# First attention: Q and K rows held as two 16-bit parts each, scores by three 16-bit products, opening rows moved from two queues

## The reference

```python
xh = x.reshape(B, S, H, dh)                       # H = 16 heads, dh = 16
theta_q = xh / (1.0 + jnp.abs(w_q)) + b_q + t * phi_q
sin_q, cos_q = lookup_sin_cos(theta_q)            # table of 1024, linear in between
Q = jnp.concatenate([cos_q, sin_q], axis=-1)      # 32 wide; K alike
theta_v = xh / (1.0 + jnp.abs(w_v)) + b_v
V = cos_v + sin_v
scores = jnp.einsum('bqhd,bkhd->bhqk', Q, K) / scale
scores = jnp.where(causal, -jnp.inf, scores)
attn = jax.nn.softmax(scores, axis=-1)
out = jnp.einsum('bhqk,bkhd->bqhd', attn, V).reshape(B, S, D)
theta_out = out / (1.0 + jnp.abs(w_out)) + b_out
return cos_o + sin_o                              # x = x + this, x normalised before
```

## Time and profile before

| | |
|---|---|
| median of three runs | 1050.36 us |
| the profiled execution | 1049.52 us |
| its span (first to last instruction) | 1047.6 us |
| PE busy | 912.2 us (87%) |
| DVE busy | 716.4 us (68%) |
| ACT busy | 574.1 us (55%) |
| scores' fills, line 635, busy | 123.6 us |
| weighings, line 655, busy | 74.6 us |
| exponentials, line 542, busy | 137.5 us |

### The profile page before, as it was taken

One profiled execution on the slowest core, in us unless ns is written; L12 is line 12 of the kernel. 1 busy time (PEld: TensorE's weight loads), 2 busy tenths in 40 slices (PEclk: granted clock), 3 DMA queues, 4 the chain that ended last, 5 costly groups with the idle time before them and its releaser, 6 DMA issues. The chain is left out here.

```text
span 1047.6 us, 20337 instructions
## 1 busy us (share of the span) xinstructions
PE 912.2 (87%) x7994; PEld 561.8 (54%) x7994; DVE 716.4 (68%) x1404; ACT 574.1 (55%) x1030; POOL 299.6 (29%) x293
## 2 busy tenths in 40 slices
PE   1587989799579789999789999998799988999997
PEld 0232333333147545565456777776689974455554
DVE  7986774615678989887768889886678764344412
ACT  3478688878478553552145555554678753332410
POOL 1222333212137231000237667666153210000000
PEclk9997889899779999999989999999899999999999
DMA  5406050320131030000130000000200000000001
GB/s 153 72 1 81 1 74 8 45 38 1 50 113 41 2 131 1 2 2 1 34 131 2 3 2 2 2 2 2 71 2 2 2 2 1 1 6 16 21 1 41
DMA packets 20573, 30.34 MB, mean 29 GB/s; under 512 B 5936, under 2 KB 15870, under 8 KB 19328
## 3 DMA queue, kind: packets, MB, share of 16 engines
q1 hardware_dynamic: 18368, 26.96, 11.2%
q10 hardware_dynamic: 2112, 2.10, 0.6%
HBM read 18.56 MB, written 2.10 MB: 20 GB/s over the span
## 5 line engine op out<-in xcount | busy, mean ns | idle before, releaser
L542 ACT ACTIVATE t_pT<-t_sc 128x1536 f32<-128x1536 f32 x96 | 137.5, 1454 | 48.9 <-PE t_sc L635 48.1
L635 PE MATMUL t_sc<-t_qk 32*128 32x512 f32 (+3 forms) x768 | 123.6, 603 | 43.7 <-DMA t_qk<-t_sines 26.0
L3149 PE MATMUL f_psh<-f_h,fs_w 128*128 128x512 f16 x512 | 114.4, 379 | 1.5 <-DVE f_h L3093 1.5
L3093 DVE SCALAR_TENSOR_TENSOR f_h<-f_psh,f_h 128x512 f16<-128x512 f32 x64 | 43.8, 690 | 100.8 <-ACT f_h L3119 100.7
L635 PEld LDWEIGHTS t_sc<-t_qk 32*128 32x128 f32 x768 | 56.6, 209 | 102.3 <-ACT t_pT L542 47.0
L261 POOL TENSOR_SCALAR_AFFINE_SELECT t_pT<-t_pT 128x512 f32<-128x512 f32 x64 | 61.2, 977 | 170.5 <-ACT t_pT L542 170.3
L3119 ACT ACTIVATE f_h<-f_psh 128x512 f16<-128x512 f32 x64 | 38.2, 597 | 108.4 <-PE f_psh L3149 108.4
L2612 POOL TENSOR_SCALAR_AFFINE_SELECT r_att<-r_att 128x1024 f16<-128x1024 f16 x64 | 69.5, 1108 | 68.5 <-DVE r_att L2652 68.3
L655 PE MATMUL t_ot<-t_pT,t_v 128*17 128x512 f32 (+3 forms) x768 | 74.6, 505 | 10.1 <-DVE t_ou L394 8.5
L3149 PEld LDWEIGHTS f_psh<-f_h,fs_w 128*128 128x128 f16 x512 | 49.8, 98 | 59.0 <-issue 2.0
L1908 PE MATMUL c_pso<-ck_VO,c_pT 128*128 128x256 f16 x480 | 55.0, 273 | 1.4 <-DVE c_pT L1759 1.4
(11 more groups left out here) (510 smaller groups left out, 2056.2 us busy)
## 6 DMA issues: line engine op xcount, KB each, us to landing
t_qk<-t_cosines SPq DMA_DIRECT2D x24, 128.0 KB, 5.6
t_qk<-t_sines SPq DMA_DIRECT2D x24, 128.0 KB, 7.0
x<-in_x ACTq DMA_DIRECT2D x4, 512.0 KB, 6.8
out_x<-x SPq DMA_DIRECT2D x4, 512.0 KB, 2.9
r_rcos<-in_ret_cos SPq DMA_DIRECT2D x1, 1280.0 KB, 8.0
r_rsin<-in_ret_sin SPq DMA_DIRECT2D x1, 1280.0 KB, 10.6
t_qk<-t_cosines SPq DMA_DIRECT2D x16, 64.0 KB, 2.3
t_qk<-t_sines SPq DMA_DIRECT2D x16, 64.0 KB, 2.3
```

The costliest lines, as they stand in the source:

```text
L542: a.activation(pT[:, at:at + 3, :].rearrange("p a s -> p (a s)"), sc[s % 2][:], ACT.Exp, scale=CURVE * CURVE / math.sqrt(2 * DH)).then_inc ...
L635: last = t.matmul(sc[s % 2][:, 512 * k + at:512 * k + at + w], qk[r, g % 3, 1, P * i:P * i + P], qk[r, g % 3, 0, q0:q0 + w], start=(part = ...
L3093: v.scalar_tensor_tensor(dst[:, 1], psh[:, i % BANKS, :], 0.0, dst[:, 0], ALU.max, ALU.subtract).then_inc(lo_done, 1)
L3149: last = mm(psh[:, i % BANKS, :], l, r, start=(k == 0), stop=(k == len(todo) - 1))
```

## The change

`cosines` and `sines` are still formed in 32 bits. Each is then split into two 16-bit parts, the value rounded to 16 bits and what is left over, in the new tiles `cos_parts` and `sin_parts`; `qk` holds both parts of each row (the bytes stay the same). A score is the sum of three 16-bit products: high by high, high of K by low of Q, low of K by high of Q.

- In group 0 ACT makes the rounded parts, in the later groups DVE does; DVE subtracts in all.
- In group 0 the four transfers of quad 0's sines are issued by ACT, those of the second half behind exp 1; all others stay with SP.
- `turn_step(1)` moves from before exp 8 to before exp 3 of quad 0, and `prepare(1)` with its rest moves ahead of `post_v(0)` and `pre_v(1)`. Statistics of the second batch, the row gains and `variances(1)` change places around `post_qk(0, 1)`.
- `turn_step(n)` on ACT now waits for `bent` instead of the transfers; `post_qk(n)` waits for the transfers out of the parts before it writes them.

```diff
-        qk = sb("qk", [P, 3, 2, S])
+        qk = sb("qk", [P, 3, 2, 2, S], F16)
+        cos_parts, sin_parts = sb("cos_parts", [P, 2, 2, S], F16), sb("sin_parts", [P, 2, 2, S], F16)
...
-        TURN_AT = {(0, 8): 1, (2, 2): 2, (4, 2): 3}
+        TURN_AT = {(0, 3): 1, (2, 2): 2, (4, 2): 3}
...
+        def moves(g, c, lo, hi):
+
+            for hh in range(4):
+                at, to = 64 * (g % 2) + 16 * hh, 32 * hh + 16 * c
+                yield qk[to:to + 16, g % 3, :, :, lo:hi], (cos_parts, sin_parts)[c][at:at + 16, :, :, lo:hi]
...
             for h in range(2):
                 for g in range(2):
                     for c in range(2):
-                        if g == 0:
-                            sp.wait_ge(bent, 2 * pieces_of(0, h) - 1 + c)
+                        if g == 0 and c == 1:
+                            continue
+                        sp.wait_ge(bent, 2 * pieces_of(0, h) - 1 + c)
                         move(g, c, 512 * h, 512 * h + 512, moved[g] if h or g else first)
...
             def post_qk(n, h=None):
                 f = piece(frac, h)
+                lo, hi = (0, S) if h is None else (512 * h, 512 * h + 512)
                 v.wait_ge(sin_pre, pieces_of(n, h))
-                for w, waves in ((cosines, cos_waves), (sines, sin_waves)):
+                if n:
+                    parts_free(n)
+                sides = ((cosines, cos_waves, cos_parts), (sines, sin_waves, sin_parts))
+                for w, waves, _ in sides:
                     v.wait_ge(waves, pieces_of(n, h))
-                    v.scalar_tensor_tensor(piece(w, h), f, CURVE_OFF, piece(w, h), ALU.add, ALU.mult).then_inc(bent, 1)
+                    v.scalar_tensor_tensor(piece(w, h), f, CURVE_OFF, piece(w, h), ALU.add, ALU.mult).then_inc(formed, 1)
+                if n:
+                    v.wait_ge(formed, 2 * pieces_of(n, h))
+                    for w, _, parts in sides:
+                        v.tensor_copy(parts[:, :, 0, lo:hi], cut(w, lo, hi)).then_inc(rounded, 1)
+                for c, (w, _, parts) in enumerate(sides):
+                    v.wait_ge(rounded, 2 * pieces_of(n, h) - 1 + c)
+                    v.tensor_tensor(parts[:, :, 1, lo:hi], cut(w, lo, hi), parts[:, :, 0, lo:hi], ALU.subtract).then_inc(bent, 1)
...
+            sums(1, 0, 3, 4)
+            sums(1, 1, 4, TB)
 
             for h in range(2):
...
                 if h == 0:
                     post_qk(0, 0)
-            sums(1, 0, 3, 4)
-            sums(1, 1, 4, TB)
+            post_qk(0, 1)
+            variances(1)
             v.wait_ge(s_row, 16 * 4)
             row_gains(0, 0, 1, slice(0, 128))
-            post_qk(0, 1)
-            variances(1)
             pre_v(0)
+            prepare(1)
+            prepare_rest(1)
+            post_v(0)
             row_gains(0, 0, 1, slice(128, D))
+            pre_v(1)
             row_gains(1, 2, 3, slice(0, D))
             v.wait_ge(rs_ready, 2)
             v.wait_ge(mean_ready, 2)
             normalise(TB, 2 * TB, xn_next)
-            post_v(0)
-            pre_v(1)
-            prepare(1)
-            prepare_rest(1)
...
+            def move_sines(h):
+
+                a.wait_ge(bent, 2 * pieces_of(0, h))
+                for dst, src in moves(0, 1, 512 * h, 512 * h + 512):
+                    a.dma_start(dst, src).then_inc(moved[0] if h else first, 16)
...
-            waves_qk(0, 0)
-            waves_qk(0, 1)
+            for h in range(2):
+                waves_qk(0, h)
+                for c, (w, parts) in enumerate(((cosines, cos_parts), (sines, sin_parts))):
+                    a.wait_ge(formed, 2 * pieces_of(0, h) - 1 + c)
+                    a.copy(parts[:, :, 0, 512 * h:512 * h + 512],
+                           w[:].rearrange("p (k s) -> p k s", k=2)[:, :, 512 * h:512 * h + 512]).then_inc(rounded, 1)
+                if h == 0:
+                    move_sines(0)
             for g in range(QUADS):
                 for e in range(EXPS):
...
                     exp_step(EXPS * g + e)
+                    if (g, e) == (0, 1):
+                        move_sines(1)
...
-                for part in range(2):
+                for part, (of_k, of_q) in itertools.product(range(2), ((0, 0), (0, 1), (1, 0))):
                     for slot, h, k in chunks:
...
-                            last = t.matmul(sc[s % 2][:, 512 * k + at:512 * k + at + w], qk[r, g % 3, 1, P * i:P * i + P],
-                                            qk[r, g % 3, 0, q0:q0 + w], start=(part == 0), stop=True, skip_group_check=True)
+                            last = t.matmul(sc[s % 2][:, 512 * k + at:512 * k + at + w], qk[r, g % 3, 1, of_k, P * i:P * i + P],
+                                            qk[r, g % 3, 0, of_q, q0:q0 + w], start=(part == 0 and of_k == of_q == 0),
+                                            stop=(of_k == 1), skip_group_check=True)
```

More of the change, by code:

```diff
@@ L1 @@
 from contextlib import ExitStack
+import itertools
 import math
@@ L155, in table_attention @@
         cos_pre, sin_pre, cos_waves, sin_waves, bent = (sem(n) for n in ("cos_pre", "sin_pre", "cos_waves", "sin_waves", "bent"))
+        formed, rounded = sem("formed"), sem("rounded")
         first, moved = sem("first"), [sem(f"moved{k}") for k in range(3)]
@@ L217, in move @@
             def move(g, c, lo, hi, done):
[L219 to L222, removed]
+                for dst, src in moves(g, c, lo, hi):
+                    sp.dma_start(dst, src).then_inc(done, 16)
             for h in range(2):
@@ L349, in post_qk, with cut, parts_free @@
                 f = piece(frac, h)
+                lo, hi = (0, S) if h is None else (512 * h, 512 * h + 512)
                 v.wait_ge(sin_pre, pieces_of(n, h))
-                for w, waves in ((cosines, cos_waves), (sines, sin_waves)):
+                if n:
+                    parts_free(n)
+                sides = ((cosines, cos_waves, cos_parts), (sines, sin_waves, sin_parts))
+                for w, waves, _ in sides:
                     v.wait_ge(waves, pieces_of(n, h))
-                    v.scalar_tensor_tensor(piece(w, h), f, CURVE_OFF, piece(w, h), ALU.add, ALU.mult).then_inc(bent, 1)
+                    v.scalar_tensor_tensor(piece(w, h), f, CURVE_OFF, piece(w, h), ALU.add, ALU.mult).then_inc(formed, 1)
[6 more added lines that the diff above has]
+                    v.tensor_tensor(parts[:, :, 1, lo:hi], cut(w, lo, hi), parts[:, :, 0, lo:hi], ALU.subtract).then_inc(bent, 1)
+            def cut(w, lo, hi):
+                return w[:].rearrange("p (k s) -> p k s", k=2)[:, :, lo:hi]
+            def parts_free(n):
+                for g in (2 * n - 2, 2 * n - 1):
+                    v.wait_ge(moved[g % 3], moves_of(g))
+                if n == 1:
+                    v.wait_ge(first, 16 * 8)
             def pre_v(n):
@@ L476, in _ @@
             prepare_rest(1)
+            post_v(0)
+            row_gains(0, 0, 1, slice(128, D))
+            pre_v(1)
+            row_gains(1, 2, 3, slice(0, D))
+            v.wait_ge(rs_ready, 2)
+            v.wait_ge(mean_ready, 2)
+            normalise(TB, 2 * TB, xn_next)
             for g in range(1, QUADS):
@@ L524, in turn_step @@
                 if n:
[L525 to L528, removed]
+                    a.wait_ge(bent, 2 * pieces_of(n - 1))
                 lo, hi = (0, S) if h is None else (512 * h, 512 * h + 512)
```

## The result

The changed kernel took 1058.01 us (median of 14 runs, 1053.80 to 1062.26), the kernel before 1049.67 in the same comparison (14 runs, 1045.51 to 1055.47). The ratio is 1.0071, 95% interval [1.0048, 1.0095]: slower. The forecast was 1063, in a range of 1050 to 1076. The profiled execution took 1058.36 us (span 1056.6), against 1049.52 (span 1047.6).

A forecast was written before the change was run, and what follows sets the result against it. TensorE was taken as the bound in plain stretches, the vector engine then TensorE in odd quads; 5.5 + 6.9 + 4.9 + 5.0 - 1.75 - 2.2 - 5.5 = +12.9 on 1049.52 gave 1062.4, forecast 1063 us, range 1050 to 1076.

The forecast's parts named there:

- opening, up to T: Up to T, the start of the first odd quad's cosine activation: +3.4 to +8.7 us later, taken as +5.5.
- stop, quad 1: First odd quad, slot 2: TensorE waits for the vector engine to empty the second output bank; stage 6.9 us later.
- stop, quad 3: Second odd quad: TensorE waits for the same bank, after a slack of 2.4 us; stage 4.9 us later.
- clock behind the stops: After both new stops TensorE runs 8 us at half clock: 2.5 us lost twice, 5.0 in all.
- fills after quads 1, 3, 5: Shorter score fills give back 2.2 us after g = 2, 1.75 after g = 4, 5.5 from g = 5 on.
- stage end: End of the first attention, at about 275 us before the change: +12.9 us as the sum of all terms.
- The four operations: Two casts and two subtractions of 128x2048 in post_qk on the vector engine, ahead of the bank's emptying: 7.3 us.
- the third load bare: Rival: each fill's third weight load isn't overlapped, 0.2 to 0.3 us per fill; no gain, 1074 us; chance 0.08.
- The six slots: TensorE's weighing slots in the opening, before T: 5.35 us at full clock, at most 10.7 at half.
- The second queue saving nothing: Opening: issuing sines' transfers from the scalar engine too saves nothing, as it is busy when the data come.
- Rows of quad 6: Rows of Q and K arrive later at quad 6, where it is close: counted as nothing, up to 1 us.
- The faster rival: Slot 2 of quads 1 and 3: the vector engine's four operations hide, so -9 us, 1041 us; chance 0.12.

The follow-up runs named there:

- bank_first: Changed kernel with front_o(g-1, 1) moved ahead of pre_v(n+1) in odd quads; 1048.79 us, ratio 0.9975 to the kernel before.
- value_between: Changed kernel with post_v(0) moved between prepare(1) and prepare_rest(1) in the opening; 1059.90 us, ratio 1.0088 to the kernel before.

## Why the prediction was right, and where it was off

The direction, the place and the mechanism were right; the forecast was 5 us too high, and the terms of the stage were 8 too high, of which a late start of the profiled execution hides 2.5. By its own terms, in the profiled executions:

| term | predicted | measured | from |
|---|---|---|---|
| opening, up to T | +5.5 | +5.0, of it 2.5 not the kernel's | T 84.44 against 79.46 |
| stop, quad 1 | +6.9 | +7.0 | T to slot 2: 24.73 against 17.76 |
| stop, quad 3 | +4.9 | +4.8 | 24.53 against 19.72 |
| clock behind the stops | +5.0 | -0.3 | see below |
| fills after quads 1, 3, 5 | -2.2, -1.75, -5.5 | -2.9, -0.9, -5.4 | |
| stage end | +12.9 | +7.3 | 282.58 against 275.32 |
| span | | +9.0 | 1056.6 against 1047.6 |

**The step that failed is the clock behind the stops.** The prediction took 8 us at half clock behind each stop, after the 10 us seen at 146 to 156: 4 us of lost work less six shorter fills. It was 4.4 and 3.6 us, some 2 us of lost work each, and the shorter fills paid for that: from slot 2 to the activation of the next rotation it took 10.83 us against 10.84 in quad 1 (predicted 2.5 more) and 10.55 against 10.85 in quad 3. In the row that the prediction used, the stop was 4.2 us long and the clock fell only at its end:

```profile
145.50:146.00 0.50, 0.00 (x0) 0.00 (x0) 0.47 (x2) 0.50 (x1) 0.00 (x0) 0.98 1.11 180
```

So all of the 10 us at 0.50 lay in work there (9.71 of 10 us busy). In the two new, longer stops the clock fell 1.8 and 4.2 us after TensorE stopped, and 5.8 and 3.2 us at 0.50 passed while it stood anyway. The Trainium skill ("TensorE: Matmul & The Clock Gate", Part 1) says that the window in which activity is watched is free-running. By that rule the time at half clock behind a stop depends on where the stop falls, which would fit the three stops; no run here isolates it.

**Where the stage and the total differ.** The stage ends 7.3 us later and the span 9.0. The 1.7 us arise in stages that the change doesn't touch. From the stage end to the end of the span the thirteen profiled executions take between 771.4 and 776.8 us with the same code, so 1.7 is within what single executions differ by. Since 2.5 us of the profiled opening is not the kernel's and the medians still differ by 8.3, the profiled execution and the medians don't add up to better than some 3 us.

**The four operations** took 8.0 us in quad 1 and 7.6 in quad 3 by starts (predicted 7.3): casts 1.23 and 1.65 in quad 1, 1.23 and 1.22 in quad 3, subtractions 2.71. The cast was priced about right, the subtraction 0.36 too low. The bank was predicted free at T + 24.6 and was at T + 24.67; that it is so close is in part luck. In quad 1 the four took 0.7 us and `post_v` 0.4 us more than assumed, and `pre_v` 1.2 us less than before (7.57 against 8.74).

**The fills** were forecast at 0.89 and 1.6, and were 0.82 and 1.46. The rule of the Trainium skill ("TensorE: Matmul & The Clock Gate", Part 3), that loads overlap only with matmuls of another row group, would have left the third load bare. The trace does not agree. Nine products and nine loads in 0.82 us show nothing bare, and a fourth product adds 0.22, one matmul of 512 columns; the rival falls.

**The opening** was the second term that was mis-sized, 5.5 us against 2.5 of the kernel's own; the late start made it look right. Exp 2's fill was forecast at 45.9 and came at 45.55, or 43.1 without the late start. The reason failed: the prediction put the sines' issue on the scalar engine behind exps 0 and 1, and the trace shows the four issues running beside them, the first at 40.56, as soon as the subtraction had ended (40.53; lines below). The first weighing, forecast 8.1 us later, came 7.75 later, 5.3 without the late start. The six slots took 8.20 us against 5.35 (the clock is at 0.50 until about 72 us), between the two levels of the prediction. The wait of 4.75 us is gone, as predicted, and from the slots' end to T it took 9.4 us (predicted 10.3). So T was 2.5 us later by the kernel itself, under the lower end of 3.4. The second queue saving nothing of the total was right, for the wrong reason.

**Rows of quad 6** were late by 2.19 us ("up to 1"). **The faster rival** needed the four operations to hide; they did not, but `bank_first`, where TensorE finds the bank empty, shows about what it would have given, 1048.8, not 1041, since late rows and the even quads' banks are next in line.

## What to carry to other kernels

An operation made cheaper on one engine is paid for in the queue of the engine that does the splitting: read what stands in that queue behind the new instructions, and who waits for it. Here 8 us of vector work ahead of one small operation that empties a bank stopped TensorE twice, for 15 us in all, and made the stage 12 us later, more than the 9 us that the faster fills gave back. Moving that operation ahead of work that nobody waits for took 9 us back; with the other moves in the same queue a loss of 0.7% became a gain of 1.3%, and the kernel before gets 0.5% from those moves too. When a stop is removed, read the next one before counting the gain: `bank_first` got 9 of 15 us, and one of the next moves gave nothing until another was taken out.

## What the runs showed of the hardware

Transfers on the scalar engine's queue are issued while activations run. ACTq is the queue's own row:

```profile
40.56 0.59 ACTq L597 DMA_DIRECT2D t_qk<-t_sin_parts  x1
40.58 1.45 ACT L567 ACTIVATE t_pT<-t_sc 128x1536 f32<-128x1536 f32 x1
41.18 1.28 ACTq L597 DMA_DIRECT2D t_qk<-t_sin_parts  x2
41.93 1.45 ACT L567 ACTIVATE t_pT<-t_sc 128x1536 f32<-128x1536 f32 x1
```

The issues stand behind both exponentials in the code, and the first begins 0.02 us before the first of them.

Three heads' 16-bit products of 32 rows run side by side, three deep, in 0.82 us, so a fill costs 0.22 us per product and some 0.16 besides.

How long a vector operation of 128x2048 takes goes with what GpSimd does when it starts. In the changed kernel GpSimd zeroes diagonal blocks from 92.01 to 99.66: the cast that starts at 91.10 takes 1.23 us, the one at 92.24 takes 1.65, both subtractions 2.71. In `value_between` the zeroing ends at 92.41, between the two subtractions:

```profile
92.01 7.65 POOL L268 TENSOR_SCALAR_AFFINE_SELECT t_pT<-t_pT 128x512 f32<-128x512 f32 x4 [8.19 <-ACT t_pT L567]
```

```profile
84.40 8.01 POOL L268 TENSOR_SCALAR_AFFINE_SELECT t_pT<-t_pT 128x512 f32<-128x512 f32 x4 [7.79 <-ACT t_pT L567]
91.83 2.71 DVE L371 TENSOR_TENSOR t_cos_parts<-t_cosines,t_cos_parts 128x2048 f16<-128x2048 f32 x1
94.47 2.28 DVE L371 TENSOR_TENSOR t_sin_parts<-t_sines,t_sin_parts 128x2048 f16<-128x2048 f32 x1
```

It is so in all nine traces with the parts (54 casts, 54 subtractions): begun while GpSimd was zeroing, a cast took 1.54 to 1.66 us and a subtraction 2.71 or 2.72; begun while it was idle, 1.22 to 1.23 and 2.28. No run changed GpSimd's work alone, so that GpSimd is the cause is not shown. By these rows the four operations would take about 7.0 us with GpSimd idle (twice 1.23 and twice 2.28, an estimate), against 8.0 in quad 1.
